# The passage from attention into the shared expert: another order on four engines, and the row conversion split between ScalarE and VectorE

## The reference

```python
h = take(W.T, x)                                    # embedding
h = h + attn(layernorm(h), w_qkv, w_out, b_out, gamma, beta)   # six layers
z = layernorm(h)
gate = z @ gate_w                                   # 8 scores a token
w = softmax over the two best scores, else 0
out = sum_e swiglu(z, ew1[e], ew2[e], ew3[e]) * w[e] + swiglu(z, sw1, sw2, sw3)
return h + out                                      # swiglu: (z@w1) * sigmoid(z@w1) * (z@w2) @ w3
```

## Time and profile before

| | us |
|---|---|
| median of 3 timed runs | 1394.66 |
| lowest and highest of them | 1389.75, 1396.74 |
| the profiled execution, its own time | 1381.39 |
| its span, first to last instruction | 1379.6 |
| TensorE busy in the span | 1235.7 |

### The profile page before, as it was taken

The page is one execution under the profiler, slowest core; times in us unless marked ns, Lnnn a source line. Parts: engine busy times, 40 slices in busy tenths (PEclk is TensorE's granted clock), DMA queues, the critical chain, the costliest instruction groups (busy, mean ns, idle before and its releaser), DMA issues. The chain is left out here.

```text
span 1379.6 us, 35753 instructions
## 1 busy us (share of the span) xinstructions
PE 1235.7 (90%) x10490; PEld 1011.1 (73%) x10491; DVE 1021.6 (74%) x2668; ACT 862.5 (63%) x2363; POOL 837.1 (61%) x863
## 2 busy tenths in 40 slices
PE   4415889999999999999999999897999999999994
PEld 3314677888888888888888888764565888777773
DVE  2236899999999999999998999885766455555552
ACT  2214678899889988998898788765553233333330
POOL 3057787777677767776787877645754134334443
PEclk8657999999999999999999999998999999999997
DMA  9943655655554554335333675533443465565542
GB/s 338 368 151 92 135 145 130 161 126 134 120 128 97 130 137 101 66 68 117 79 74 61 122 152 91 91 48 93 132 135 122 95 93 86 84 89 89 89 71 32
DMA packets 366103, 161.22 MB, mean 117 GB/s; under 512 B 296880, under 2 KB 350416, under 8 KB 366032
## 3 DMA queue, kind: packets, MB, share of 16 engines
q1 hardware_dynamic: 333200, 121.50, 39.2%
q0 software_dynamic: 19104, 25.32, 10.3%
q10 hardware_dynamic: 13728, 13.63, 2.8%
HBM read 44.60 MB, written 42.24 MB: 63 GB/s over the span
## 5 line engine op out<-in xcount | busy, mean ns | idle before, releaser
L916 PE MATMUL bank<-hT,Wc 128*128 128x256 f16 x2304 | 286.3, 275 | 43.6 <-DMA hT<-hhl 29.2
L916 PEld LDWEIGHTS bank<-hT,Wc 128*128 128x128 f16 x2304 | 226.8, 99 | 71.8 <-issue 44.0
L730 POOL TENSOR_TENSOR h0b<-h0b,rows 128x512 f32<-128x512 f32 x80 | 101.4, 1267 | 137.9 <-DVE h0b L1534 85.8
L844 POOL DMA_INDIRECT out_rows<-h0b,payin x50 | 78.0, 1560 | 128.1 <-DVE h0b L1845 67.2
L916 PE MATMUL bank<-Wc,MT 128*128 128x256 f16 x1152 | 142.7, 274 | 12.7 <-DVE MT L1580 12.7
L916 PE MATMUL bank<-khl,eqT 128*128 128x256 f16 x1152 | 141.3, 272 | 1.5 <-DVE khl L1592 0.3
L916 PE MATMUL bank<-Wc,hT 128*128 128x256 f16 x1152 | 142.1, 273 | 0.0
L1017 PE MATMUL bank<-xTg,Wall 128*128 128x256 f16 x1200 | 136.9, 275 | 3.1 <-DMA payin<-slot_x 3.1
L916 PEld LDWEIGHTS bank<-Wc,MT 128*128 128x128 f16 x1152 | 112.5, 98 | 28.9 <-issue 11.6
L1017 PEld LDWEIGHTS bank<-xTg,Wall 128*128 x1200 | 118.1, 99 | 18.4 <-issue 3.6
L916 PEld LDWEIGHTS bank<-khl,eqT 128*128 128x128 f16 x1152 | 109.5, 97 | 22.7 <-issue 9.2
(11 more groups left out here) (204 smaller groups left out, 2770.2 us busy)
## 6 DMA issues: line engine op xcount, KB each, us to landing
Wall<-in_L_tok_W SPq DMA_DIRECT2D x25, 512.0 KB, 7.9
emb<-Wall ACTq DMA_DIRECT2D x25, 512.0 KB, 10.0
Wall<-in_L_ffn_ew SPq DMA_DIRECT2D x24, 512.0 KB, 4.1
Wc<-Wn SPq DMA_DIRECT2D x40, 128.0 KB, 2.7
Wst<-in_L_attn_w_qkv SPq DMA_DIRECT2D x12, 384.0 KB, 3.6
h_rows<-Wall SPq DMA_DIRECT2D x8, 512.0 KB, 3.1
X<-h_rows POOLq DMA_DIRECT2D x8, 512.0 KB, 6.4
out_rows<-X SPq DMA_DIRECT2D x8, 512.0 KB
```

The costliest lines, as they stand in the source:

```text
L730: pool.tensor_tensor(xn[:, :, :], xn[:, :, :], row(0), ALU.mult).then_inc(s_hg, 1)
L844: pool.indirect_dma_start(out=out_rows, out_offset=bass.IndirectOffsetOnAxis(ap=index, axis=0), in_=source, in_offset=None, compute_op=ALU ...
L916: last = mm(to, lhs(a, k, o), moving, start=(i == 0 and k == 0), stop=(i == 2 and k == 1))
```

## The change

On TensorE, ScalarE and VectorE the lists of groups 0 to 5 are written anew; GpSimd loses the low halves from group 4 on. In words:

- VectorE takes two gated products of group 0 before and after the last attention sum, and makes all low halves of group 0, ahead of the choice of group 0.
- TensorE takes `up_shared(1, 0)` between the scores of group 0 and of group 1, and `down_shared(0)` before `up_shared(1, 1)`.
- The choices of groups 2, 3 and 4 move from groups 1, 2 and 3 into groups 2, 2 and 3; `stats_of(7)` moves behind group 1.
- `high(g)` for groups 4 to 7 moves from ScalarE's start of group g-3 to the middle of group g-2, right behind `high_shared(g-2, 1)`, and `normed(g)` to the end of group g-3.
- `low(g)` for groups 4 to 7 moves from GpSimd to VectorE, behind `rank(g-1)` in group g-2.

```diff
--- before.py
+++ after.py
@@ -827,17 +827,13 @@
             low(2)
             root(6)
             low(3)
+            scatter_x(0)
             root(7)
-            scatter_x(0)
             pool.memset(padl[:, :], 0).then_inc(s_padz, 1)
             pool.wait_ge(s_padz, 2)
             pool.iota(padl[:, D:D + 1].bitcast(i32), pattern=[[0, 1]], base=TOK, channel_multiplier=1).then_inc(s_padt, 1)
-            scatter_x(1)
-            low(4)
-            for g in range(2, NG):
+            for g in range(1, NG):
                 scatter_x(g)
-                if g + 3 < NG:
-                    low(g + 3)
 
             def add_rows(source, index, sem_):
 
@@ -1098,25 +1094,35 @@
             for freed in (s_eqlo, s_klo, s_vlo, s_mlo, s_plo):
                 pe.wait_ge(freed, ITEMS)
             gates_of(0)
+            pe.wait_ge(s_xT[1], 16 * GT)
+            up_shared(1, 0)
             gates_of(1)
-            for g in range(1, NG):
+            down_shared(0)
+            up_shared(1, 1)
+            ranks(0)
+            down_shared(1)
+            ranks(1)
+            up_shared(1, 2)
+            up_shared(1, 3)
+            gates_of(2)
+            for g in range(2, NG):
                 up_shared(g, 0)
-                if g == 1:
-                    ranks(0)
+                if g == 3:
+                    gates_of(4)
                 down_shared(2 * g - 2)
                 up_shared(g, 1)
-                if g == 1:
-                    ranks(1)
+                if g == 2:
+                    ranks(2)
                 down_shared(2 * g - 1)
-                if g == 1:
-                    gates_of(2)
+                if g == 2:
+                    gates_of(3)
                 elif g + 1 < NG:
                     ranks(g + 1)
                 up_shared(g, 2)
-                if g == 1:
-                    ranks(2)
                 up_shared(g, 3)
-                if g + 2 < NG:
+                if g == 2:
+                    ranks(3)
+                elif g + 2 < NG:
                     gates_of(g + 2)
 
 
@@ -1355,30 +1361,43 @@
             high_shared(0, 0)
             high_shared(0, 1)
             silu_of(2, 0)
+            silu_of(3, 1)
             high_shared(0, 2)
-            silu_of(3, 1)
+            high_shared(0, 3)
+            silu_of(HC, 0)
             share_exp(0)
-            high_shared(0, 3)
+            normed(3)
+            high(3)
             share_exp(1)
-            for g in range(1, NG):
-                if g > 1 and g + 1 < NG:
+            silu_of(HC + 1, 1)
+            high_shared(1, 0)
+            high_shared(1, 1)
+            silu_of(HC + 2, 0)
+            high_shared(1, 2)
+            silu_of(HC + 3, 1)
+            high_shared(1, 3)
+            normed(4)
+            for g in range(2, NG):
+                if g == 2:
+                    share_exp(2)
+                elif g >= 4 and g + 1 < NG:
                     share_exp(g + 1)
                 silu_of(HC * g, 0)
-                if g == 1:
-                    normed(3)
-                    high(3)
-                elif g + 3 < NG:
+                if g == 3:
+                    share_exp(4)
+                silu_of(HC * g + 1, 1)
+                high_shared(g, 0)
+                high_shared(g, 1)
+                if g + 2 < NG:
+                    high(g + 2)
+                if g == 2:
+                    share_exp(3)
+                silu_of(HC * g + 2, 0)
+                high_shared(g, 2)
+                silu_of(HC * g + 3, 1)
+                high_shared(g, 3)
+                if g + 3 < NG:
                     normed(g + 3)
-                    high(g + 3)
-                silu_of(HC * g + 1, 1)
-                for c in range(HC):
-                    if g == 1 and c == 2:
-                        share_exp(2)
-                        normed(4)
-                        high(4)
-                    if c >= 2:
-                        silu_of(HC * g + c, c % 2)
-                    high_shared(g, c)
 
             silu_of(2 * SHP, 0)
             silu_of(2 * SHP + 1, 1)
@@ -1636,7 +1655,6 @@
                           ITEMS - 2: (5, 0, 4), ITEMS - 1: (6, 2, 4)}
             late_stats = {ITEMS - 5: (1, 0, 2), ITEMS - 4: (2, 0, 2), ITEMS - 3: (3, 0, 2), ITEMS - 2: (4, 0, 4), ITEMS - 1: (6, 0, 2)}
             item_loop(dve, one, AHEAD + 1, unroll=ITEMS - NB)
-            add(ITEMS - 1)
 
 
             count = [2]
@@ -1786,19 +1804,40 @@
                 gated(i, half)
                 glow(i, i % 2, half)
 
+            def low(g):
+
+                dve.wait_ge(s_fxhi, g + 1 - EARLY)
+                dve.wait_ge(s_fxlo, g)
+                V.tensor_tensor(xhl(g % ROWS, 1), h0b[:, 1 - g % 2, :, :], xhl(g % ROWS, 0), ALU.subtract).then_inc(s_fxlo, 1)
+
             low_shared(0, 0)
+            gated_shared(0, 2)
+            add(ITEMS - 1)
             low_shared(0, 1)
-            gate_shared(0, 2)
+            gated_shared(0, 3)
+            low_shared(0, 2)
+            low_shared(0, 3)
             choose(0)
-            gate_shared(0, 3)
+            gated_shared(1, 0)
             choose(1)
+            share(0, 0)
+            gated_shared(1, 1)
+            rank(0)
+            low_shared(1, 0)
+            share(1, 1)
+            low_shared(1, 1)
+            rank(1)
+            gate_shared(1, 2)
+            gate_shared(1, 3)
             stats_of(7)
-            for g in range(1, NG):
-                if g > 1 and g + 1 < NG:
+            for g in range(2, NG):
+                if g == 2:
+                    choose(2)
+                elif g >= 4 and g + 1 < NG:
                     choose(g + 1)
                 gated_shared(g, 0)
-                if g == 1:
-                    rank(0)
+                if g == 3:
+                    choose(4)
                 share(2 * g - 2, 0)
                 if g == NG - 1:
                     tile_bases()
@@ -1808,12 +1847,11 @@
                 if g == NG - 1:
                     word_starts()
                     word_places()
-                if g == 1:
-                    rank(1)
                 share(2 * g - 1, 1)
                 low_shared(g, 1)
-                if g == 1:
-                    choose(2)
+                if g == 2:
+                    rank(2)
+                    choose(3)
                 elif g + 1 < NG:
                     rank(g + 1)
                 if g == NG - 2:
@@ -1821,12 +1859,14 @@
                     pair_counts()
                 if g == NG - 1:
                     word_digits()
+                if g + 2 < NG:
+                    low(g + 2)
                 gate_shared(g, 2)
-                if g == 1:
-                    rank(2)
                 if g == NG - 2:
                     pair_bases()
                 gate_shared(g, 3)
+                if g == 2:
+                    rank(3)
                 if g == NG - 2:
                     tile_counts()
 
```

## The result

The change makes the kernel slower by 20 us. The kernel before took 1393.41 us in the median (four runs, 1389.75 to 1396.74), the changed one 1413.38 (four runs, 1412.47 to 1414.04): a ratio of 1.0151, 95% interval 1.0134 to 1.0167. The forecast was 1404 with 1389 to 1413 as its range, so the direction held and the size did not: twice the loss that was forecast, just outside the range. The profiled execution of the changed kernel took 1413.52 us, its span 1411.5.

What follows compares the result with a forecast made beforehand. TensorE, busy 1235.7 of 1379.6 us, was taken to bound the kernel. A loss of 24.3 from mid-group row conversion less 14.4 given back after attention made +9.9, so 1394.7 + 9.9 = 1404.6, range 1389 to 1413.

Steps and rivals of the forecast that it cites:

- Part 2: Mid-group row conversion for groups 5, 6 and 7: TensorE waits 5.7 for transposes plus 2.4 low clock each, 24.3 lost.
- The low clock: In the up_shared behind each transpose wait of groups 5 to 7: TensorE at low clock, 2.4 us lost each time.
- The rival of sooner landing: Transposes of groups 5 to 7 land in 2.7, not 6.3: 1392; chance 0.2, shared with the clock staying up.
- Part 1: From the end of attention to the scores of group 5: the new lists remove TensorE idle time, giving back 14.4.
- the passage: Stretch from the scores of group 0 to TensorE reaching those of group 5, where waits for VectorE would shrink.
- The walk: Stepping TensorE's new list from group 0's scores by instruction times and waits, reaching group 5's scores at 986.5.
- 1000.89: Start of group 5's scores in the first profile, taken as the old time against the new 986.5.
- 13.1 with the first down's 2.65: Last stretch of TensorE's list before group 5's scores: down, up, down, counts and two ups, added to reach 986.5.
- the product behind the low half: VectorE's gated product after the rows' low half: late at no cost, with 2 us left before the next group's up_shared.
- The 13 us that I carried over: Whole kernel: the median of runs stood 13 above the profiled execution, and this was added to the forecast unchanged.
- The passage gains and nothing is lost: Rows' high half ready early, so transposes land before TensorE asks in groups 5 to 7: -14.4, 1380; chance 0.13.
- The change doesn't do in the passage what it says: down_shared(0) or the counts still wait for VectorE; only 7.2 given back, 17 slower, 1412; chance 0.07.

Runs made afterwards that it cites:

- the second profile of before: The kernel before, unchanged, profiled once more: 1394.15 us, with 81.3 us from the scores of group 0 to those of group 5.
- without scatters: GpSimd's scatters of groups 0 to 3 left out: of the changed kernel 1402.54 us (1.0070 of before), of the kernel before 1385.94 us (0.9937).
- the first profile: The profiled execution of the kernel before that the prediction argued from, no edit: 1381.39 us, 73.2 from the scores of group 0 to those of group 5.
- early rows: The changed kernel with the rows' high half behind the group's first silu, their low half behind VectorE's first sum: 1391.41 us, 0.9990 of before.
- the plain writes: The changed kernel with GpSimd's scatters of groups 0 to 3 replaced by plain writes to unread slots: 1404.88 us, 1.0095 of before.
- the run with half of the scatters: The early rows kernel with only the first choice of each token of groups 0 to 3 scattered: 1374.97 us.

## Why the prediction was wrong, step by step

**Part 2 was right, and a little small.** The waits are 6.87, 6.84 and 6.99 for 5.7, because the four transposes land 7.7 us behind their start (1006.34 to 1014.03) and not 6.3; I had put the landing 1.1 behind the last issue. VectorE's low half took 1.23, as taken. The low clock costs 4.45, 5.07 and 4.06, the pitches of the three `up_shared`, less 2.59 each: 5.8 in all, for 7.2. Together 20.7 + 5.8 = 26.5, for 24.3. The rule on a loop that waits for a DMA in each round (the Trainium skill, "TensorE: Matmul & The Clock Gate", section "HAM oscillation") is borne out: the clock was 0.57, 0.50 and 0.63 over the three `up_shared`. The rival of sooner landing is out: 7.7, not 2.7. The Trainium skill, "Advanced Engine Details and Errata", section "X-Bar Transpose (TRN2)", has transposes as fast as regular DMAs; the 7.7 for four of 128 KB is far above the 2.7 of one plain transfer of that size, but plain ones of 512 KB, as much as the four, land in 3.1 to 10.0 in the kernel before, so no run here compares like with like.

**Part 1 failed, at the step "Part 1 gives back 14.4".** Against the second profile of before, the passage gives back 81.3 - 79.0 = 2.3. Two things were wrong in that one term. The walk charged TensorE with its instructions and its waits alone, and put what runs beside it at nothing; its list was good (60.2 measured without scatters, 58.8 walked), but beside GpSimd's scatters the same list takes 79.0. And its other end, 1000.89, came from an execution that had no such hold-up; the second profile reaches it 8.1 later in the passage, so the comparison was with a passage that usual executions, as far as the second profile stands for them, do not have. Where nothing is held up on either side, the term comes near: 73.2 - 60.2 = 13.0. The two kernels without scatters differ by 64.9 - 60.2 = 4.7 only, since there the old passage loses its longest wait, the one for the scatters of group 0.

Two slips in the working bear on nothing. "13.1 with the first down's 2.65" should read 13.4, and 986.5 was added up with it. And the product behind the low half, had it not waited, would have had 0.4 us left and not 2 (1015.68 + 1.25 + 0.7 = 1017.63 against 1018.05).

**The account.** Against the second profile of before: passage -2.3; from group 5's scores to the experts' first product 98.25 for 74.96, +23.3, that is part 2's 26.5 less the 4.4 that the second profile of before loses there to the same hold-up (74.96 against 70.55 in the first profile), with 1.2 left over; expert phase -1.8; start -0.1. The sum, +19.1, is the difference of the spans, 1411.5 - 1392.4. The 13 us that I carried over from the profiled execution to the median were therefore not a constant: 12.5 of them lay between 928 and the experts, in the stretch that the change rewrites. With -2.3 for -14.4 my sum would have been 1394.7 + 22 = 1417. That the time lies only 0.4 above the range is luck, since this one term missed by 12.

**The rivals.** "The passage gains and nothing is lost" named the right lever (early rows start the transposes in time) but not its price: at 1391 that kernel only equals the one before, since the passage gained nothing. "The change doesn't do in the passage what it says" had 1412, near the time, and the wrong reason: the low halves were ready, `down_shared(0)` started at 933.66.

**What is shown and what is not.** Shown: the stops vanish with the scatters, with half of them, and in part with pauses between them; they move when the scatters move. So the scatters are needed for them. But they are not enough: the first profile of before has as many, in runs as long, and no stop. What else it takes is not shown, nor which part of the chip the stops pass through. In the second profile and in the changed kernel the stops and late semaphores come with missing records of semaphore updates: the semaphore of one buffer's scatters has 256 updates in the first profile of before, 79 in the second, 126 in the changed kernel. Counted over the passage, at 16 updates a scatter, 495 of 528 are recorded in the first profile, 141 of 528 in the second, 96 of 528 in the changed kernel, and 512 of 528 with the plain writes, which had no stops. Yet the run with half of the scatters has only 111 of 288, and no stops: records can be missing without them. The Trainium skill, "NOTIFIC — the notification-queue block", section "7.1 Overflow: three behaviours, one of which stalls the engine", says that the block which writes trace records can, in one of three settings, hold up the engine that makes them when a queue is full, and in another drops the record. If that is at work here, part of the hold-up belongs to the recording; no run here tells it from a hold-up that a run without recording would have too.

## What to carry to other kernels

Ask whether the profiled execution is a usual one before taking a walk from it: when the timed runs are 1% longer, find where that lies, for a change in that stretch will be measured against the longer version. A list of instructions that fits without waits is a lower bound only; look at what other engines issue beside it, above all long runs of indirect writes, and try pauses in them (they gave 0.5% here). An experiment that leaves work out also leaves out the waits for it; name them before comparing. And a conversion that another engine's DMA must follow belongs as early in the loop as its inputs allow, not behind a wait that the consumer itself releases.

## What the runs showed of the hardware

- GpSimd's indirect writes of 128 rows of 1040 bytes, 1.27 us each: runs of eight to sixteen held TensorE up in ten profiled executions (in the changed kernel 0.7 us a matmul in place of 0.1, semaphores up to 10.6 us late, beginning 5 to 14 us into a run and ending 1 to 3 us behind it), and in the first profile of before they did not. Runs of four did not (0.1 us lost of 55).
- The same rows by plain writes of GpSimd are issued in 0.54 us each, and TensorE did not stop beside them.
- Four transposes of a group, 128 KB each, took 5.16 us to issue, and TensorE went on 7.7 us behind their start.
